# Stage 0 of an eight-stage network: softplus kept in PSUM, one scan per tile, two tiles per GpSimd product, stage 4's weights in another place, and every engine's order from a table

## The chip, the cores and the metric

The kernel runs on one core of one Trainium2 chip. The metric is the device time of one execution in microseconds. The median of three runs of the kernel before is 1385.8 us (1383.31 to 1387.94).

## The reference, cut to what matters

An activation of 8 sequences of 256 tokens with 128 features goes through four layers of two parts, so eight stages, 0 to 7, in float32. Each stage computes x = norm(x + stage(x)); the steps of that norm are "0.e", "f" and "g" below. Stage 0 is a state-space mixer and a small MLP, 1, 2, 4 and 6 are attentions of four kinds (1 with a mixture of experts behind it), 3 an MLP with binarized weights, 5 and 7 mixtures of experts. The change bears on the arithmetic of stage 0 alone:

```
u     = silu(conv(in_proj(ln(x))))            # and z, the same with other weights
delta = softplus(dt_proj(x_proj_dt(u)) + b)
B, C  = x_proj_B(u), x_proj_C(u)              # 16 states
h[t]  = exp(delta[t] * A) * h[t-1] + delta[t] * u[t] * B[t]      # 128 channels x 16 states, h = 0 before t = 0
y     = sum over states of h * C  + u * Dp
x1    = x + out_proj([y, z])
out   = x1 + (gelu(ln(x1) @ w1 + b1) @ w2 + b2)
x     = norm(x + out)
```

## The kernel before, in words

The 2048 tokens are four chunks (c = 0 to 3) of 512 tokens, two sequences of 256 each. A chunk's eight stages run one after another. Three lanes of scratch space (arena) hold the chunks in flight: chunk 0, chunk 1, and chunks 2 and 3, which share the third lane. The scratch is SBUF; the eight PSUM banks of 128 x 512 floats are given out over all stages.

Each stage is a list of steps, named like "0.st", and each step has parts, each on one engine (P is TensorE, A ScalarE, V VectorE, G GpSimd, D the DMA queue SP). `order_of_steps` runs a planner while the program is being built: with `PARTS`, an assumed duration for each part, and the tables `AHEAD`, `URGENT`, `HASTE` and `STAY` it picks one part after another, and gives each engine a fixed list and each result its bank. `OPENS` and `HELD` say from which part to which a step holds a bank. The engines then run their lists in order, and wait on semaphores for one another. What is behind a waiting instruction on an engine waits with it.

Stage 0 for one chunk: the norm (0.n), the first convolution on TensorE (0.in), B and C (0.bc, two banks evicted to SBUF by ScalarE), and softplus (0.dt, 0.ln, 0.dr, 0.du): ScalarE makes |v|, relu(v), exp(-|v|), tanh(|v|/2) and a logarithm in SBUF, VectorE corrects the rounding of 1 + exp with an add L1772 and three scalar_tensor_tensor (L1775), adds, and multiplies by u (two L1769). The product delta * u goes to DRAM (0.wr) and comes back repeated, one 128 x 512 tile for each of 16 groups of eight channels and 16 states (0.rp). For each group q GpSimd multiplies the tile by B (0.db, L2315). TensorE spreads delta over the states, four groups at a time into four banks (0.da, decays, named A to D), and ScalarE turns each into exp(delta * A) in its bank. VectorE scans (0.st): two instructions of 256 elements, one per sequence, L1946 and L1947, with the decays in PSUM and the products in SBUF. Then h is multiplied by C (0.hc), by VectorE (a L1769, h and C in SBUF) or by GpSimd (L2319) as the planner decides. TensorE sums over states (0.ac). For chunk 2 the first two groups are spread by TensorE instead of the DMA (0.rb). The end: 0.y (out projection and residual), 0.m (second norm, in place of s0(c, 2)), 0.h (w1 and gelu), 0.x on GpSimd, which adds b2 to x1 (L2336; b2 is spread over partitions by the step 0.b) and then x once more (L2340), 0.o (w2, 16 matmuls, and a VectorE add), 0.e (the norm of stage 1's input).

Line numbers that the rows show: 1064 and 1068 are TensorE's helpers for a matmul and for transposes, 1514 ScalarE's helper, 1769, 1772 and 1775 VectorE's helpers for tensor_tensor, tensor_scalar and scalar_tensor_tensor, 2328 the experts' product on GpSimd (two tiles wide in stage 5), 1010 the repeated copies, 982 the weight loads.

W[0] holds stage 0's weights from column 0, and later stage 4's: `load` of stage 4 waits in the DMA queue until the last chunk (3) has passed 0.e and until products made ahead of time for stage 4 (4.l to 4.st) are in DRAM; then it loads W[0] from column 2048 and the products into columns 0 to 2047.

Of the kernel before, what the change touches and what calls it, by code (L numbers as in the profile page):

```python
# [24 lines left out]
    [("lng", 1), ("lnb", 1), ("cxb", 1), ("czb", 1), ("dtb", 1), ("dp", 1), ("ln2g", 1), ("ln2b", 1),  # L25
     ("alog", 16), ("win", 256), ("xbc", 256), ("xdt", 128), ("dtw", 128),
# [13 lines left out]
W_AT = {3: WMAX - 1160, 2: WMAX, 4: 2048}  # L40
# [7 lines left out]
FIRST0 = 1816  # L48
# [48 lines left out]
TILED = {"0.da": "r", "0.rb": "r", "1.sc": "r", "5.bb": "r", "0.f": "r", "0.b": "r", "3.b": "r", "1.a": "r", "0.ac": "c", "1.pv": "c", "4.pv": "c",  # L97
# [36 lines left out]
HELD = {("0.ac", 0): [("Y", 0, ("0.y", 0, 0), 4, 1)], ("1.pv", 0): [("Y", 0, ("1.y", 0, 0), 8, 1)],  # L134
# [10 lines left out]
for _u in range(UNITS):  # L145
# [48 lines left out]
def stage_steps(s, c):  # L194
# [42 lines left out]
    if s == 0:  # L237
# [6 lines left out]
        add("0.du", 0, ("0.ln", 0), ("0.dr", 0))  # L244
        add("0.wr", 0, ("0.du", 0))
        add("0.in", 1, ("0.bc", 0))
        for q in range(16):
            by = "0.rb" if c == BEGIN[0] and q < BEGIN[1] else "0.rp"
            if by == "0.rb":
                if q == 0:  # L250
                    add(by, 0, ("0.du", 0))
            else:
                add(by, q, ("0.wr", 0), *([("0.ac", (q - STATES) // 4)] if q >= STATES else []))
            if q % 4:
                add("0.da", q, ("0.da", q - 1))
            else:
                add("0.da", q, ("0.du", 0), ("0.a", 0, PREP), *([("0.st", q - 3)] if q >= 4 else []))
            if by == "0.rp":
                add("0.db", q, (by, q), ("0.bc", 0))
            add("0.st", q, ("0.da", q), ("0.db", q) if by == "0.rp" else (by, 0), ("0.bc", 0), *([("0.st", q - 1)] if q else []))  # L260
            add("0.hc", q, ("0.st", q))
# [6 lines left out]
        add("0.x", 0, ("0.m", 0), ("0.b", 0, PREP))  # L268
        add("0.o", 0, ("0.x", 0), *[("0.h", j) for j in range(4)])
# [79 lines left out]
def weight_steps():  # L349

    loads = [("load", s, 0, [("f" if q else "0.e", 0, c, q) for q in OVER[s] for c in range(NC)]
# [2190 lines left out]
```

## Time and profile before

| | us |
|---|---|
| median of 3 runs | 1385.8 |
| the profiled execution | 1385.3 |
| its span, first to last instruction | 1383.5 |
| TensorE busy | 1280.2 |
| VectorE busy | 941.4 |
| ScalarE busy | 896.0 |
| GpSimd busy | 789.7 |

The mean granted TensorE clock is 0.968 of full speed. The busy times overlap: five engines work side by side, so no sum of them is the span. An instruction of an engine can seem to overlap with the next by some 80 ns; the step from start to start is then what it costs. A row "engine line waited for another" is idle time of the first ended by the second.

### The profile page before, as it was taken

What the parts mean: (1) busy time and instruction counts of PE and PEld (TensorE: products, weight loads), DVE (VectorE), ACT (ScalarE), POOL (GpSimd) and SP (SyncE); (2) the same over time, 40 slices, a digit from 0 to 9 for tenths busy, and PEclk for the clock granted to TensorE, in tenths of its full rate; (3) what the DMA queues carried; (4) which work ended last, traced back from release to release, by engine and by line L of the source; (5) the groups of instructions that cost most, each with busy time, mean ns of one, the idle gap of its engine ahead of it and who ended that gap; (6) DMA issues with size and microseconds to landing.
All of it is one profiled execution on the core that took longest, in us unless ns stands there. A gap on an engine that the chain in (4) does not pass through costs nothing.

```text
span 1383.5 us, 26286 instructions
## 1 busy us (share of the span) xinstructions
PE 1280.2 (93%) x8734; PEld 909.6 (66%) x8734; DVE 941.4 (68%) x3661; ACT 896.0 (65%) x2495; POOL 789.7 (57%) x876
## 2 busy tenths in 40 slices
PE   8577988899977889999999999999999999999997
PEld 4233655567644666677767867777777867886665
DVE  5989868677568677757563663485988659864253
ACT  6736689787474679767787676556568664775231
POOL 2998666576378556466556756355435325450534
PEclk9868899899998999999999999999999999999999
DMA  8742000101141100110010001301020030001431
GB/s 285 193 122 76 9 9 2 55 2 55 55 103 28 37 1 1 55 65 1 1 63 1 1 1 63 125 1 62 2 81 1 1 93 1 2 2 70 115 91 32
DMA packets 23109, 67.86 MB, mean 49 GB/s; under 512 B 2336, under 2 KB 9120, under 8 KB 20672
## 3 DMA queue, kind: packets, MB, share of 16 engines
q1 hardware_dynamic: 22976, 66.20, 15.2%
q8 instruction: 70, 1.15, 0.3%
q14 instruction: 63, 0.52, 0.1%
HBM read 62.85 MB, written 3.34 MB: 48 GB/s over the span
## 4 chain that ended last, share of the span: by engine, by line
PE 65%; DVE 11%; POOL 9%; ACT 8%; issue 5%; DMA 2%; SPq 0%; POOLq 0%; DVEq 0%; ACTq 0%
PE bank L1064 57%; PE bank L1068 8%; ACT arena L1514 6%; POOL arena L2315 3%; DMA arena<-cf 2%; DVE arena L1769 2%; DVE arena L2261 2%; POOL arena L2386 1%; DVE arena L2254 1%; DVE arena L2012 1%; POOL arena L2385 1%; POOL arena L2328 1%; DVE arena L1947 1%; DVE arena L2010 1%; DVE stats L1783 1%
## 5 line engine op out<-in xcount | busy, mean ns | idle before, releaser
L1514 ACT ACTIVATE arena<-arena 128x256 f32<-128x256 f32 (+4 forms) x808 | 357.9, 447 | 64.7 <-DVE arena L2012 32.5
L1514 ACT ACTIVATE arena<-bank 128x512 f32<-128x512 f32 (+3 forms) x355 | 190.7, 563 | 230.3 <-PE bank L1064 144.5
L1064 PE MATMUL bank<-XT,W 128*128 128x512 f32 (+1 forms) x752 | 290.2, 523 | 1.0 <-DVE arena L1775 0.6
L1064 PEld LDWEIGHTS bank<-W,arena 128*128 128x128 f32 x1888 | 231.5, 193 | 52.5 <-issue 39.4
L1064 PE MATMUL bank<-W,arena 128*128 128x128 f32 (+1 forms) x1888 | 243.4, 279 | 6.2 <-POOL arena L2328 3.1
L2385 POOL TENSOR_TENSOR arena<-arena 128x256 f32<-128x256 f32 x192 | 117.6, 613 | 220.8 <-DVE arena L2018 220.0
L1064 PE MATMUL bank<-arena 128*32 128x128 f32 (+8 forms) x2912 | 228.0, 336 | 16.2 <-ACT arena L1514 7.4
L2328 POOL TENSOR_TENSOR arena<-arena 128x512 f32<-128x512 f32 (+1 forms) x108 | 170.8, 1601 | 93.7 <-DVE arena L1769 39.0
L1064 PEld LDWEIGHTS bank<-arena 128*32 128x32 f32 (+4 forms) x2912 | 154.8, 153 | 81.1 <-issue 45.2
L1068 PE MATMUL bank<-CF,arena 128*128 128x128 f32 x1312 | 182.1, 279 | 23.9 <-POOL arena L2386 10.7
L2386 POOL TENSOR_TENSOR arena<-arena 128x512 f32<-128x512 f32 x192 | 199.7, 1040 | 0.0
L1068 PEld LDWEIGHTS bank<-CF,arena 128*128 128x128 f32 x1312 | 150.7, 143 | 67.1 <-issue 49.5
L1064 PE MATMUL bank<-arena,W 128*128 128x512 f32 (+3 forms) x412 | 161.1, 679 | 34.0 <-DVE arena L1947 22.0
L1064 PEld LDWEIGHTS bank<-XT,W 128*128 128x128 f32 x752 | 134.0, 190 | 83.3 <-issue 77.0
L1514 ACT ACTIVATE arena<-bank,W 128x512 f32<-128x512 f32 (+1 forms) x192 | 109.5, 616 | 67.4 <-PE bank L1064 56.0
L1514 ACT ACTIVATION_READ_ACCUMULATOR arena<-arena 128x1 f32 x768 | 145.4, 189 | 0.0
L2024 DVE COPY arena<-bank 128x512 f32<-128x512 f32 x155 | 103.2, 682 | 60.7 <-PE bank L1068 60.2
L1064 PEld LDWEIGHTS bank<-arena,W 128*128 128x128 f32 (+1 forms) x412 | 59.7, 207 | 108.4 <-issue 94.5
L1769 DVE TENSOR_TENSOR arena<-bank,arena 128x512 f32<-128x512 f32 x98 | 65.9, 686 | 84.1 <-PE bank L1064 68.8
L1514 ACT ACT_TABLE_LOAD x75 | 96.2, 1283 | 25.2 <-PE bank L1064 12.5
L2012 DVE CUSTOM_DVE_ANT_0 arena<-bank,CB 128x256 f32<-128x256 f32 x256 | 107.3, 419 | 0.0
L2010 DVE CUSTOM_DVE_ANT_0 arena<-bank,CB 128x128 f32<-128x128 f32 x256 | 73.2, 286 | 40.2 <-PE bank L1064 37.2
(138 smaller groups left out, 1700.5 us busy)
## 6 DMA issues: line engine op xcount, KB each, us to landing
arena<-rws SPq DMA_DIRECT2D x8, 2048.0 KB, 7.4
arena<-rep SPq DMA_DIRECT2D x62, 256.0 KB, 5.9
arena<-rws SPq DMA_DIRECT2D x4, 1792.0 KB, 6.6
W<-w SPq DMA_DIRECT2D x2, 2124.0 KB, 8.6
arena<-rws SPq DMA_DIRECT2D x8, 384.0 KB, 10.4
W<-w SPq DMA_DIRECT2D x1, 2692.0 KB, 9.3
XT<-wkq SPq DMA_DIRECT2D x4, 512.0 KB, 8.3
W<-w SPq DMA_DIRECT2D x1, 2005.0 KB, 15.5
```

What stands on the lines that cost most here:

```text
L1064: return e.matmul(o, lhsT, rhs, start=start, stop=stop, skip_group_check=True)
L1068: ins = e.transpose(bank[b.i][:, j * 128:j * 128 + s.shape[0]], s, cst("ident"))
L1514: return e.activation(o, a, func, **kw)
L1769: return e.tensor_tensor(o, a, b, op)
L2010: e.tensor_tensor_reduce(px[:, j * 384:j * 384 + 128], bank[b.i][:, 0:128], bias[:, 0:128], -1.0, 3.4e38, ALU.add, ALU.min, nm[:, 2 * j:2 ...
L2012: e.tensor_tensor_reduce(px[:, j * 384 + 128:(j + 1) * 384], bank[b.i][:, 128:384], bias[:, 128:384], -1.0, 3.4e38, ALU.add, ALU.min, nm[: ...
L2024: e.tensor_copy(third(s, c, n), bank[b.i][:, :]).then_inc(done[b.i], 1)
L2261: own(e.match_replace(R[:, qs], e8, src[:, qs], TAKEN))
L2315: e.tensor_tensor(h, h, s0(c, 8), ALU.mult).then_inc(has["dB"], 1)
L2328: e.tensor_tensor(h, h, w, ALU.mult).then_inc(has["gw"], 1)
L2385: e.tensor_tensor(px[:, :, 0:128], px[:, :, 0:128], rec[:, :, 0:1].to_broadcast([128, 2, 128]), ALU.mult)
L2386: e.tensor_tensor(px[:, :, 128:384], px[:, :, 128:384], rec[:, :, 1:2].to_broadcast([128, 2, 256]), ALU.mult).then_inc(has["pn"], 1)
```

## The change

What it does, part by part:

- Softplus: exp(-|v|), the three corrections and the last add are written in the PSUM bank of 0.dt, which is held until a new step 0.dc. ScalarE's 0.dc copies delta from there to SBUF, all but the first column of each sequence, where VectorE has put a zero (memset).
- One scan of 512 elements instead of two of 256: the decay at the first column of the second sequence is zero, since delta is zero there and the Exp skips these columns (`later`).
- C: evicted to SBUF as before, for GpSimd, but the bank is held until the last 0.ac, and VectorE's C product reads C from the bank.
- 0.db: one GpSimd product for two groups, 128 x 1024, B broadcast over the two. It waits for both tiles.
- 0.x and 0.b go. 0.o starts with four matmuls with a single row that put b2 in its bank, and 0.y's VectorE part has a second instruction that leaves 2x + out_proj, which is x + x1, in X, and 0.o adds that.
- Stage 4's weights lie in W[0] from column 2087 to 4519, over those of stage 0's convolution, B, C and delta; w1, w2 and others of stage 0 lie in front. The load waits for 0.in, part 1, and 0.dt of all chunks and no longer for 0.e.
- 1.km: either half may go to ScalarE or VectorE.
- The order: the planner's tables are gone. `TURNS` has 3891 turns, one for each part (negative: the second of two engines that could do it), and each engine takes its parts in the order of their turns. Banks are still given out by the same walk. `PARTS` has new numbers.

The chunks begin stage 0 in the order 2, 0, 1, 3 before and 2, 1, 0, 3 after.

```diff
-W_AT = {3: WMAX - 1160, 2: WMAX, 4: 2048}
+W_AT = {3: WMAX - 1160, 2: WMAX, 4: 4135}
-HELD = {("0.ac", 0): [("Y", 0, ("0.y", 0, 0), 4, 1)], ("1.pv", 0): [("Y", 0, ("1.y", 0, 0), 8, 1)],
+HELD = {("0.dt", 0): [("b", 0, ("0.dc", 0, 0), 1, 1)], ("0.bc", 0): [("c", 0, ("0.ac", 3, 0), 1, 1)], ("0.ac", 0): [("Y", 0, ("0.y", 0, 0), 4, 1)], ("1.pv", 0): [("Y", 0, ("1.y", 0, 0), 8, 1)],
...
-    loads = [("load", s, 0, [("f" if q else "0.e", 0, c, q) for q in OVER[s] for c in range(NC)]
+    loads = [("load", s, 0, [need for q in OVER[s] for c in range(NC) for need in ([("f", 0, c, q)] if q else [("0.in", 1, c, 0), ("0.dt", 0, c, 0)])]
...
+    turns = {g: [] for g in "PAVGD"}
+    rows = {k: iter(v) for k, v in TURNS.items()}
     for x in all_steps:
+        for p, (engines, one, other) in enumerate(x.parts):
+            turn = next(rows[x.name, x.s, x.c])
+            x.parts[p] = (engines[0], one) if turn > 0 else (engines[1], other)
+            turns[x.parts[p][0]].append((abs(turn), x, p))
+    for g in "PAVGD":
+        turns[g].sort(key=lambda y: y[0])
...
+        def later(a):
+            return a.rearrange("p (b l) -> p b l", b=2)[:, :, 1:256]
...
                 elif name in ("0.o", "3.o"):
...
+                    if s == 0:
+                        for j in range(4):
+                            mm(ps[:, j * 128:(j + 1) * 128], cst("one", 1), wt(0, "b2", 0, 1), j == 0, False)
...
-                    act(s0(c, 13), s0(c, 12), ACT.Exp, scale=-1.0).then_inc(has["sf_e"], 1)
+                    act(bank[b.i][:, :], s0(c, 12), ACT.Exp, scale=-1.0).then_inc(has["sf_e"], 1)
...
+                elif name == "0.dc":
+                    b = u("b", "0.dt", c)
+                    on.wait_ge(*after("du", "0.du", c))
+                    act(later(step0(c, 0)), later(bank[b.i][:, :]), ACT.Copy).then_inc(done[b.i], 1)
...
-                    ts(s0(c, 14), s0(c, 13), 1.0, None, ALU.add).then_inc(has["sf_f"], 1)
+                    ts(s0(c, 14), ps[:, :], 1.0, None, ALU.add).then_inc(has["sf_f"], 1)
...
-                    own(tt(step0(c, 0), s0(c, 13), s0(c, 12), ALU.add))
-                    on.wait_ge(*own.last())
-                    tt(step0(c, 1), step0(c, 0), s0(c, 6), ALU.mult).then_inc(has["du"], 1)
+                    own(e.memset(step0(c, 0).rearrange("p (b l) -> p b l", b=2)[:, :, 0:1], 0.0))
+                    own(tt(ps[:, :], ps[:, :], s0(c, 12), ALU.add))
+                    on.wait_ge(*own.last())
+                    tt(step0(c, 1), ps[:, :], s0(c, 6), ALU.mult).then_inc(has["du"], 1)
...
-                    own(e.tensor_tensor_scan(h[:, 0:256], bank[a.i][:, 0:256], h[:, 0:256], 0.0, ALU.mult, ALU.add))
-                    e.tensor_tensor_scan(h[:, 256:512], bank[a.i][:, 256:512], h[:, 256:512], 0.0, ALU.mult, ALU.add
-                                         ).then_inc(done[a.i], 1)
+                    e.tensor_tensor_scan(h, bank[a.i][:, :], h, 0.0, ALU.mult, ALU.add).then_inc(done[a.i], 1)
...
-                    tt(ring0(c, n), ring0(c, n), s0(c, 16), ALU.mult).then_inc(has["hc_v"], 1)
+                    tt(ring0(c, n), ring0(c, n), bank[cc.i][:, :], ALU.mult).then_inc(has["hc_v"], 1)
...
-                    tt(s0(c, 2), bank[b.i][:, :], rows(0, c), ALU.add).then_inc(done[b.i], 1)
+                    own(tt(s0(c, 2), bank[b.i][:, :], rows(0, c), ALU.add))
+                    stt(rows(0, c), rows(0, c), 2.0, bank[b.i][:, :], ALU.mult, ALU.add).then_inc(done[b.i], 1)
...
-                    h = ring0(c, n)
-                    on.wait_ge(*repeated(c, n))
+                    h = ar(c, 3640 + (2 * n % STATES) * 512, 1024).rearrange("p (k t) -> p k t", k=2)
+                    on.wait_ge(*repeated(c, 2 * n))
+                    on.wait_ge(*repeated(c, 2 * n + 1))
                     on.wait_ge(*emptied(u("b", "0.bc", c)))
-                    e.tensor_tensor(h, h, s0(c, 8), ALU.mult).then_inc(has["dB"], 1)
+                    e.tensor_tensor(h, h, s0(c, 8).unsqueeze(1).to_broadcast([128, 2, 512]), ALU.mult).then_inc(has["dB"], 1)
```

## Rows read from the trace of the kernel before

**Rows 1.** page: busy time per engine; tenths busy in 40 slices

```profile
PE 1280.2 (93%) x8734; PEld 909.6 (66%) x8734; DVE 941.4 (68%) x3661; ACT 896.0 (65%) x2495; POOL 789.7 (57%) x876
...
PE   8577988899977889999999999999999999999997
```

**Rows 2.** stretches: length, busy us (count) per engine, PEclk, DMA share, GB/s

```profile
20.00:150.00 130.00, 94.39 (x454) 45.27 (x453) 116.78 (x196) 80.37 (x122) 110.56 (x80) 0.83 0.48 128
150.00:200.00 50.00, 43.01 (x344) 30.55 (x347) 35.44 (x154) 39.67 (x126) 32.42 (x34) 0.86 0.03 11
200.00:385.00 185.00, 168.90 (x1376) 115.08 (x1372) 132.43 (x606) 142.13 (x446) 112.47 (x124) 0.97 0.08 32
385.00:500.00 115.00, 93.24 (x561) 63.66 (x560) 83.80 (x225) 69.47 (x136) 80.12 (x71) 0.93 0.19 51
500.00:1350.00 850.00, 837.47 (x5826) 627.33 (x5825) 552.97 (x2417) 549.49 (x1646) 434.51 (x549) 1.00 0.11 37
```

**Rows 3.** waits, 50 to 100 us: total us, times, longest

```profile
ACT bank L1514 <- PE bank L1064: 23.5, 5, 8.1
...
DVE arena L1946 <- ACT bank L1514: 4.6, 1, 4.6
```

**Rows 4.** chain of waits, in time: start us, length us, what

```profile
38.54 11.08 POOL arena L2315 x7
...
403.08 14.06 POOL arena L2315 x10
```

**Rows 5.** VectorE forms, 20 to 150 us: xcount | busy us, mean ns

```profile
L1769 DVE TENSOR_TENSOR arena<-arena 128x512 f32<-128x512 f32 x31 | 32.4, 1053 | 1.6 <-ACT arena L1514 0.7
...
L1775 DVE SCALAR_TENSOR_TENSOR arena<-arena 128x512 f32<-128x512 f32 x9 | 11.6, 1293 | 0.7
...
L1769 DVE TENSOR_TENSOR arena<-bank,arena 128x512 f32<-128x512 f32 x4 | 2.7, 674 | 4.1 <-PE bank L1064 4.1
...
L1775 DVE SCALAR_TENSOR_TENSOR arena<-arena,W,bank 128x512 f32<-128x512 f32 x2 | 1.5, 732 | 0.6 <-issue 0.6
```

**Rows 6.** timeline of VectorE: start us, length us

```profile
39.63 5.70 DVE L1769 TENSOR_TENSOR arena<-arena 128x512 f32<-128x512 f32 x4
...
58.71 0.66 DVE L1769 TENSOR_TENSOR arena<-arena 128x512 f32<-128x512 f32 x1
59.29 0.68 DVE L1946 TENSOR_TENSOR_SCAN arena<-bank,arena 128x256 f32<-128x256 f32 x1
```

**Rows 7.** GpSimd by form, 20 to 150 us

```profile
L2315 POOL TENSOR_TENSOR arena<-arena 128x512 f32<-128x512 f32 x46 | 69.3, 1535 | 0.0
L2319 POOL TENSOR_TENSOR arena<-arena 128x512 f32<-128x512 f32 x21 | 27.6, 1329 | 20.7 <-DVE arena L1947 20.7
...
L2340 POOL TENSOR_TENSOR arena<-arena,X 128x512 f32<-128x512 f32 x2 | 2.9, 1438 | 0.2
```

**Rows 8.** all forms, whole span

```profile
L2328 POOL TENSOR_TENSOR arena<-arena 128x1024 f32<-128x1024 f32 x32 | 75.1, 2365 | 10.5 <-ACT arena L1514 10.5
...
L1514 ACT ACTIVATE arena<-bank 128x512 f32<-128x512 f32 x311 | 178.4, 595 | 212.1 <-PE bank L1064 139.4 <-PE bank L1068 71.8
...
L1514 ACT ACTIVATE bank<-bank,am 128x512 f32<-128x512 f32 x64 | 44.3, 750 | 34.1 <-PE bank L1064 34.0
```

**Rows 9.** VectorE and GpSimd by form, 385 to 480 us

```profile
L1769 DVE TENSOR_TENSOR arena<-arena 128x512 f32<-128x512 f32 x12 | 12.2, 1017 | 2.0 <-ACT arena L1514 1.5
...
L2315 POOL TENSOR_TENSOR arena<-arena 128x512 f32<-128x512 f32 x16 | 22.1, 1409 | 0.4 <-DMA arena<-rep 0.4
```

**Rows 10.** timelines of the DMA queue (SPq) and TensorE

```profile
393.23 22.37 SPq L1010 DMA_DIRECT2D arena<-rep  x16
477.36 0.35 SPq L982 DMA_DIRECT2D W<-w  x1
...
49.48 2.09 PE L1064 MATMUL bank<-arena,W 32*128 32x512 f32 x8 [2.93 <-ACT arena L1514]
...
484.70 3.79 PE L1064 MATMUL bank<-bw,arena 128*128 128x128 f32 x32
```

More of the change, by code:

```diff
@@ L46 @@
 FIRST = 148
-FIRST0 = 1816
+LATE0 = 1924
 CONSTB = [("mask", 384)]
@@ L244, in stage_steps @@
         add("0.du", 0, ("0.ln", 0), ("0.dr", 0))
+        add("0.dc", 0, ("0.du", 0))
         add("0.wr", 0, ("0.du", 0))
@@ L256, in stage_steps @@
             else:
[L257 to L260, printed above, removed]
+                add("0.da", q, ("0.dc", 0), ("0.a", 0, PREP), *([("0.st", q - 3)] if q >= 4 else []))
+            if by == "0.rp" and q % 2:
+                add("0.db", q // 2, (by, q - 1), (by, q), ("0.bc", 0))
+        for q in range(16):
+            by = "0.rb" if c == BEGIN[0] and q < BEGIN[1] else "0.rp"
+            add("0.st", q, ("0.da", q), ("0.db", q // 2) if by == "0.rp" else (by, 0), ("0.bc", 0), *([("0.st", q - 1)] if q else []))
             add("0.hc", q, ("0.st", q))
@@ L267, in stage_steps @@
             add("0.h", j, ("0.m", 0))
-        add("0.x", 0, ("0.m", 0), ("0.b", 0, PREP))
-        add("0.o", 0, ("0.x", 0), *[("0.h", j) for j in range(4)])
+        add("0.o", 0, *[("0.h", j) for j in range(4)])
         add("0.e", 0, ("0.o", 0))
@@ L489, in __init__ @@
         self.parts, self.at = parts_of(name, n), 0
-        self.open, self.tail, self.since, self.behind = 0, 0.0, LANDS.get((name, c), 0.0), []
+        self.open, self.since, self.behind = 0, LANDS.get((name, c), 0.0), []
 def order_of_steps():
@@ L523, in order_of_steps @@
             x.open += 1
-    done_tails = set()
-    def tail(x):
-        stack = [x]
-        while stack:
-            y = stack[-1]
-            todo = [z for z in y.behind if z not in done_tails]
-            if todo:
-                stack += todo
-                continue
-            stack.pop()
-            y.tail = sum(p[1] + HOP[p[0][0]] for p in y.parts) + max((z.tail for z in y.behind), default=0.0)
-            done_tails.add(y)
-    for x in all_steps:
-        if x not in done_tails:
-            tail(x)
+    turns = {g: [] for g in "PAVGD"}
+    rows = {k: iter(v) for k, v in TURNS.items()}
+    for x in all_steps:
+        for p, (engines, one, other) in enumerate(x.parts):
[4 more added lines that the diff above has]
+        turns[g].sort(key=lambda y: y[0])
     order = {g: [] for g in "PAVGD"}
     free = dict.fromkeys("PAVGD", 0.0)
-    ready = {g: [] for g in "PAVGD"}
     banks = [(0.0, i) for i in range(8)]
@@ L546, in order_of_steps @@
     table, tiles = "e", "F"
-    def offer(since, x):
-        for g in x.parts[x.at][0]:
-            ready[g].append((since, x))
-    for x in all_steps:
-        if x.open == 0:
-            offer(x.since, x)
     def opened(x):
@@ L559, in opened @@
         return out + [(r, last, f, g) for r, o, last, f, g in HELD.get((x.name, x.n), ()) if o == x.at]
-    left = len(all_steps)
-    while left:
+    while any(turns.values()):
         best = None
         for g in "PAVGD":
-            for r, x in ready[g]:
-                t = max(r, free[g])
-                k = len(opened(x))
-                if k > len(banks):
-                    continue
-                if k:
-                    t = max(t, sorted(banks)[k - 1][0])
-                other = STAY["act"] if g == "A" and TABLE.get(x.name, table) != table else 0.0
-                turn = STAY["stay"] if g == "P" and tiled(x) != tiles else 0.0
-                key = (t - HASTE.get(x.name, 0.0) + other, -x.tail - AHEAD.get((x.s, x.c), 0.0)
-                       - URGENT.get(x.name, 0.0) - URGENT.get((x.name, x.c), 0.0) + turn)
-                if best is None or key < best[0]:
-                    best = key, g, t, r, x
-        key, g, t, r, x = best
-        for h in x.parts[x.at][0]:
-            ready[h].remove((r, x))
-        x.parts[x.at] = g, x.parts[x.at][1 if g == x.parts[x.at][0][0] else 2]
+            _, x, p = turns[g][0] if turns[g] else (0, None, 0)
+            if x is None or x.open or x.at != p:
+                continue
+            t, k = max(x.since, free[g]), len(opened(x))
+            if k > len(banks):
+                continue
+            if k:
+                t = max(t, sorted(banks)[k - 1][0])
+            if best is None or t < best[0]:
+                best = t, g, x
+        t, g, x = best
+        turns[g].pop(0)
         if g == "A" and x.name in TABLE:
@@ L606, in order_of_steps @@
         if x.at < len(x.parts):
-            offer(end + HOP[g], x)
+            x.since = end + HOP[g]
         else:
-            left -= 1
             for y in x.behind:
@@ L1159, in _ @@
                                  ring0(c, 4 * n + j), n == 0, n == 3)
+                        if n == 3 and j == 0:
+                            ins.then_inc(done[uses["c", "0.bc", c, 0].i], 1)
                     ins.then_inc(full[b.i], 1)
@@ L1592, in _ @@
                 elif name == "0.bc":
-                    for k, to in (("b", s0(c, 8)), ("c", s0(c, 16))):
-                        b = u(k, name, c)
-                        evict(b, to, bank[b.i][:, :])
+                    b, cc = u("b", name, c), uses["c", name, c, 0]
+                    evict(b, s0(c, 8), bank[b.i][:, :])
+                    on.wait_ge(*filled(cc))
+                    act(s0(c, 16), bank[cc.i][:, :], ACT.Copy).then_inc(has["c"], 1)
                 elif name == "0.f":
@@ L1615, in _ @@
                     on.wait_ge(*filled(a))
-                    act(bank[a.i][:, :], bank[a.i][:, :], ACT.Exp, scale=am[:, g:g + 1], bias=am[:, 16 + g:17 + g]).then_inc(has["dA"], 1)
+                    act(later(bank[a.i][:, :]), later(bank[a.i][:, :]), ACT.Exp, scale=am[:, g:g + 1], bias=am[:, 16 + g:17 + g]).then_inc(has["dA"], 1)
                 elif name == "0.h":
@@ L1642, in _ @@
                     on.wait_ge(*after("kq", "1.kq", c, 0))
-                    for i in (1, 3):
+                    for i in (n, n + 2):
                         ins = act(km1(c)[:, i * 512:(i + 1) * 512], s1(c, 3), ACT.Copy, scale=cst("hm")[:, i:i + 1])
@@ L1967, in _ @@
                     b = u("b", name, c)
-                    on.wait_ge(*after("x0", "0.x", c))
+                    on.wait_ge(*emptied(u("b", "0.y", c)))
                     on.wait_ge(*filled(b))
-                    tt(s0(c, 2), bank[b.i][:, :], s0(c, 2), ALU.add).then_inc(done[b.i], 1)
+                    tt(s0(c, 2), bank[b.i][:, :], rows(0, c), ALU.add).then_inc(done[b.i], 1)
                 elif name == "1.m" and p == 1:
@@ L1989, in _ @@
                     on.wait_ge(*after("kq", "1.kq", c, 0))
-                    for i in (0, 2):
+                    for i in (n, n + 2):
                         ins = ts(km1(c)[:, i * 512:(i + 1) * 512], s1(c, 3), cst("hm")[:, i:i + 1], None, ALU.mult)
@@ L2328, in _ @@
                     e.tensor_tensor(h, h, w, ALU.mult).then_inc(has["gw"], 1)
-                elif name in ("0.x", "3.x", "4.x", "6.x"):
-                    a = s0(c, 2) if s == 0 else rows(s, c)
-                    if s == 0:
-                        on.wait_ge(*after("z", "0.m", c))
-                    on.wait_ge(*emptied(u("b", {0: "0.b", 3: "3.b", 4: "4.b", 6: "6.b2"}[s], PREP)))
-                    if s:
-                        on.wait_ge(*xt_in(s, c))
-                    ins = e.tensor_tensor(v4(a), v4(a), bias_of(s).unsqueeze(1).to_broadcast([128, 4, 128]), ALU.add)
-                    if s == 0:
-                        own(ins)
-                        on.wait_ge(*own.last())
-                        ins = e.tensor_tensor(a, a, rows(0, c), ALU.add)
-                    ins.then_inc(has[f"x{s}"], 1)
+                elif name in ("3.x", "4.x", "6.x"):
+                    a = rows(s, c)
+                    on.wait_ge(*emptied(u("b", {3: "3.b", 4: "4.b", 6: "6.b2"}[s], PREP)))
+                    on.wait_ge(*xt_in(s, c))
+                    e.tensor_tensor(v4(a), v4(a), bias_of(s).unsqueeze(1).to_broadcast([128, 4, 128]), ALU.add).then_inc(has[f"x{s}"], 1)
                 elif name == "1.kq":
```

104 lines of the change are left out of this document (51 added, 53 removed), and 369 rows, old and new, of tables (AHEAD, EMITS, HASTE, OPENS).

## The prediction

> **What bounds the kernel now.** I read the busy shares first: TensorE works 93% of the span and stands at 9 tenths in every slice from the 16th to the last but one, while VectorE, ScalarE and GpSimd lie between 57 and 68% [rows 1]. So from about 500 us on TensorE's own work sets the end, and what is left to win lies where it idles. The view by stretches says where: it is busy 94.4 of 130 us in 20 to 150, 43.0 of 50, 168.9 of 185, 93.2 of 115, and then 837.5 of 850 [rows 2]. That is 35.6 + 7.0 + 16.1 + 21.8 + 12.5 = 93 us of idle time, 80.5 of it before 500. The two bad stretches (20 to 150, with stage 0 of chunks 2, 0 and 1, and 385 to 500, with that of chunk 3) also have a granted clock of 0.83 and 0.93, so part of TensorE's work went at the lower of its two levels there [rows 2].
>
> In 20 to 150 VectorE is busy 116.8 us and GpSimd 110.6 of 130 [rows 2]: this pair bounds stage 0. ScalarE waits 23.5 us for the decays' matmuls in 50 to 100, which in turn wait for scans to free their banks [rows 3]; the chain of waits runs through GpSimd's B products L2315, 11.1 us at 38.5 and 14.1 us at 403 [rows 4]. And the two engines slow each other down. VectorE's 512-wide product costs 1053 ns with both inputs in SBUF and 674 with one in PSUM; a softplus step costs 1293 ns, against 732 with a PSUM operand [rows 5]. It is not the SBUF read itself: in the timeline one such product takes 0.66 us at 58.71, but the four at 39.63 take 5.70, beside GpSimd's products of 11.08 / 7 = 1.6 us [rows 4, 6]. GpSimd's B product takes 1535 ns in the mean and its C product, of the same shape, 1329 [rows 7].
>
> **Stage 0 of the first three chunks, VectorE.** Of the 31 products with both inputs in SBUF [rows 5], 6 are those of softplus (two a chunk), so 25 are C products. All get a PSUM operand: 31 x (1.053 - 0.674) = 11.7 us. The nine L1775: 9 x (1.293 - 0.732) = 5.0. Sorted by turn, the new table gives VectorE 22 C products of these chunks (2, 11 and 9 of chunks 0, 1 and 2): 3 x 0.67 = 2.0. The scan: no row shows one of 512. The halves are 0.66 to 0.68 long but start about 0.6 apart, so they overlap by 0.08, as the scan at 59.29 starts before the product of 58.71 ends [rows 6]. One scan saves one such start: between nothing and 0.16 a tile, I take 0.07, for 46 tiles 3.2 us (bounds 0 and 7.4). Added: the add L1772 reads PSUM and cannot cost more than a product's 0.67; I put half of that on, 1.0 for three. The second residual of 0.y: 3 x 0.73 = 2.2. Three memsets of two columns, 0.2. Sum: 11.7 + 5.0 + 2.0 + 3.2 - 3.4 = 18.5 us off VectorE.
>
> **GpSimd.** 46 B products at 1.535 are 70.6 us [rows 7]. The two-tile ones have a row of their shape in stage 5, 2365 ns [rows 8]: 23 x 2.365 = 54.4, so 16.2 off. Bounds: 2 x 1.535 each, nothing off, if what slows them is not VectorE's second SBUF input, and 2.365 as the other end, which I take. 0.x goes: two of its three pairs lie in this stretch, four instructions of 1.44 [rows 7], 5.8 off. C products: 26 for 23, 4.0 on. Net 18.0 off.
>
> The Trainium skill, SBUF — State Buffer, section "SBUF: two separate sides", says that a VectorE instruction with two SBUF inputs and a GpSimd instruction that reads SBUF exclude each other, each for the whole of the other. The trace agrees (674 against 1053 ns). By this rule the end of 2.365 holds; if PSUM operands did not free GpSimd, the stage's gain below would be 8 us and not 16, and the sum 1366.
>
> The pair lose 18.5 + 18.0 = 36.5 us of work, 18.2 each if evenly shared, and both were nearly full. Against it: the copy of delta out of PSUM (0.dc) now stands between softplus and the decays, 0.6 us like any 512-wide eviction [rows 8], and the first tile of a chunk waits for a second copy and a product 1.0 us longer (2.365 - 1.329); for chunk 2, which starts alone, nothing hides that. I take 16 us. Since TensorE idles 35.6 us of this stretch and the work behind is TensorE's, they come off the end. Holding C and delta in PSUM costs no time by itself; its price is banks, a rival below. The Exp of the decays is as long as before (0.75 [rows 8]).
>
> **Stage 0 of chunk 3.** VectorE: twelve products at 1.017, 12 x (1.017 - 0.674) = 4.1 [rows 5, 9], three L1775 1.7, four fewer C products 2.7, scans 1.1, added 1.1: 8.5 off. GpSimd: 22.1 us of B products [rows 9] against 8 x 2.365 = 18.9, the pair of 0.x 2.9, four more C products 5.3 on: 0.8 off. Half of 9.3 is 4.6; I take 4, as TensorE has 21.8 us of idle time here and the chain ran through GpSimd.
>
> **Stage 4's weights.** The queue has issued chunk 3's copies by 415.6 (393.23 + 22.37), and the load waits until 477.4 for that chunk's last norm [rows 10]. Now it waits for the convolutions and delta only and can go right behind the copies, 60 us earlier; nothing stands behind it in the queue. Today TensorE has stage 1 of chunk 3 to do while it lands. In the new table stage 4 of chunks 0 and 1 opens right behind chunk 3's 0.o, which the old gate would have stalled. Alone the move is worth 0 to 6 us (a quarter of the 21.8 idle): I take 3.
>
> **TensorE's own additions.** Sixteen matmuls of 128 columns for b2. An output of 16 matmuls (32 records) takes 3.79 us [rows 10], 0.237 each: 3.8 on, 0.3 off for 0.b, all on the path: +3.5.
>
> **The order.** Chunk 1 now comes before chunk 0 in stage 0, and evictions are shared anew (59 of stage 1's 96 probability evictions on VectorE, 34 of stage 6's). The third chunk leaves stage 0 at TensorE's 92nd turn, before at the 95th, so the same work fills that stretch. A better order can reach the idle time not yet counted, 16.1 + 21.8 + 12.5 - 7 = 43 us. From 500 on TensorE already runs at 98.5% and in 200 to 500 at 87% [rows 2]. Bounds: 28 gained (two thirds of it) and 20 lost (2.4% of the 837 us given back). I take 8 gained, a fifth of the idle time of 200 to 500 and nearer to no effect than to either end, as no row shows the new order.
>
> **Sum.** The profiled execution took 1385.3 us (span 1383.5); the median of the runs is 1385.8. -16 - 4 - 3 + 3.5 - 8 = -27.5, so 1385.3 - 27.5 = 1357.8, say 1358.
>
> **Rivals.**
> 1. The order is worth more and fills two thirds of the idle time, 28 instead of 8: 1338. For it: 80 us of idle lie before 500, and the gate of stage 4 falls. Against: at the start there is no other work to fill with.
> 2. The pair's gain is absorbed and the order does nothing: TensorE waits for ScalarE instead, whose Exps stay as they are. A gain of 4 to 8, less 3.5: about 1382, hardly to be told from no change.
> 3. Slower: banks. C holds one bank per chunk through the whole scan, three with three chunks in flight; delta holds one until 0.dc, Y one. That leaves three or four of eight, so the four decay tiles of a group cannot be made while the last four are scanned. Each group then exposes its matmuls (2.09) and an Exp (0.75) [rows 8, 10], 2.9 us. The profile shows such a hand-over once, VectorE idle for 4.6 us behind ScalarE [rows 3]. Twelve groups in three chunks: 35 us over the forecast, 1393. It decides from ten groups on (27.5 / 2.9). Against it: another chunk's scans can stand in between.
> 4. The two-tile product is no cheaper: 1366, within the forecast's own range.
>
> **Chances.** Forecast with 4, a gain of 13 to 40 us: 0.58 (its own range 1345 to 1372). Rival 1: 0.16. Rival 2: 0.13, half of it within 0.3%. Rival 3: 0.13, a little of it within 0.3%. 0.3% or 4.2 us is about what a measurement of this kernel can tell. Faster 0.58 + 0.16 + 0.06 = 0.80, same 0.08, slower 0.12. The range runs from 1330 (20 off in the first stretch, 6, 5, 28 for the order, 3.5 on) to 1386, which leaves out most of rival 3.
>
> **What would show it.** No 128x512 product with both inputs in SBUF should be left on VectorE in stage 0, and the C product should cost 0.67 us; the two-tile product 2.4; the single scan 1.1 to 1.3. GpSimd should leave most of the chain before 100 us. TensorE's idle time in 20 to 150 should fall from 35.6 to about 20 us, and stage 4's load should be issued right behind chunk 3's copies. The forecast is wrong if TensorE waits for a bank in every group, if the two-tile product takes 3 us, or if the idle time from 200 on grows.

## The result, and the profile after

The changed kernel takes 1342.9 us (median of 4 runs, 1341.0 to 1346.8), the kernel before 1386.5 on the same chip: ratio 0.969, 95% interval 0.966 to 0.972, some 43 us less. The forecast was 1358 (1330 to 1386), with 0.80 on faster: the direction and the stated range held. The gain came out 16 us larger than summed, and the time lies below the 1345 to 1372 that the forecast's own mechanism was given, 5 us from rival 1's 1338; what that means for rival 1 is said at the end. The profiled execution has a span of 1340.4 us and a mean granted clock of 0.977; before it was 1383.5 and 0.968.

The page after: busy time by engine, TensorE's tenths in 40 slices, and the chain that ended last.

```profile
PE 1270.5 (95%) x8764; PEld 902.9 (67%) x8764; DVE 912.6 (68%) x3585; ACT 905.4 (68%) x2518; POOL 768.3 (57%) x844
...
PE   8779988999997989999999999999999999999997
...
PE 76%; DVE 10%; ACT 5%; issue 3%; DMA 3%; POOL 2%; SPq 0%; POOLq 0%; DVEq 0%; ACTq 0%
```

The same by stretches (length, busy us and count of PE, PEld, DVE, ACT, POOL, then the granted clock):

```profile
20.00:150.00 130.00, 108.01 (x546) 54.46 (x545) 104.26 (x183) 92.67 (x150) 97.11 (x61) 0.83 0.47 130
150.00:200.00 50.00, 44.37 (x404) 31.01 (x406) 44.15 (x207) 47.25 (x168) 35.46 (x40) 0.93 0.02 7
200.00:385.00 185.00, 173.97 (x1401) 121.45 (x1400) 138.71 (x572) 136.78 (x399) 121.42 (x129) 1.00 0.08 31
385.00:500.00 115.00, 99.15 (x649) 65.98 (x648) 86.75 (x270) 73.32 (x171) 73.51 (x70) 0.97 0.20 51
500.00:1340.00 840.00, 827.54 (x5723) 619.63 (x5721) 528.84 (x2315) 546.14 (x1622) 437.29 (x540) 1.00 0.12 38
```

TensorE's idle time is the length less its busy time. Against [rows 2] it fell from 35.6 to 22.0 in 20 to 150, from 7.0 to 5.6, 16.1 to 11.0 and 21.8 to 15.9; over the whole span from 103.3 (1383.5 - 1280.2) to 69.9. That is 33.4 of the 43.1 us. The other 9.7 are TensorE's busy time, which fell although b2's matmuls came on; the mean granted clock rose from 0.968 to 0.977, which goes with less of its work at the lower level, but no run separates the two. GpSimd's share of the chain fell from 9% to 2%.

VectorE and GpSimd in 20 to 150 (count, busy us and mean ns of one, idle time before it and what ended that), which answer [rows 5] and [rows 7]:

```profile
L2089 DVE TENSOR_TENSOR_SCAN arena<-bank,arena 128x512 f32<-128x512 f32 x48 | 56.2, 1208 | 11.0 <-ACT bank L1649 10.7 <-POOL arena L2459 0.3
L1910 DVE TENSOR_TENSOR arena<-arena,bank 128x512 f32<-128x512 f32 x22 | 14.3, 673 | 0.1
L1916 DVE SCALAR_TENSOR_TENSOR bank<-arena,bank 128x512 f32<-128x512 f32 x6 | 4.2, 696 | 0.4
```

```profile
L2459 POOL TENSOR_TENSOR arena<-arena 128x1024 f32<-128x1024 f32 x23 | 53.6, 2348 | 2.9 <-DMA arena<-rep 2.9
L2463 POOL TENSOR_TENSOR arena<-arena 128x512 f32<-128x512 f32 x26 | 32.6, 1266 | 26.4 <-DVE arena L2089 26.4
```

The C product costs 0.67 us, the two-tile product 2.35, the single scan 1.21, a softplus step 0.70: each at its forecast or within 5% of it. GpSimd's C product, an instruction that the change left alone, fell from 1329 ns to 1266.

The DMA queue after, against [rows 10]: stage 4's weights go right behind chunk 3's copies, at 418.9 and not 477.4.

```profile
396.80 21.86 SPq L1137 DMA_DIRECT2D arena<-rep  x16
418.90 0.39 SPq L1105 DMA_DIRECT2D W<-w  x1
419.39 0.38 SPq L1179 DMA_DIRECT2D W<-gs  x1
```

### The profile page after: what moved, and what is told of

Its sections match the earlier page's. It is cut to its first block, busy times and chain, and to the rows that moved or that the text cites. A ratio compares the mean times of both kernels' runs of the same rounds, so it can differ in the third digit from the quotient of the medians.

```text
span 1340.4 us, 26157 instructions
## 1 busy us (share of the span) xinstructions
PE 1270.5 (95%) x8764; PEld 902.9 (67%) x8764; DVE 912.6 (68%) x3585; ACT 905.4 (68%) x2518; POOL 768.3 (57%) x844
## 4 chain that ended last, share of the span: by engine, by line
PE 76%; DVE 10%; ACT 5%; issue 3%; DMA 3%; POOL 2%; SPq 0%; POOLq 0%; DVEq 0%; ACTq 0%
PE bank L1191 66%; PE bank L1195 10%; ACT arena L1649 5%; DVE arena L1910 2%; DVE arena L2089 2%; DMA arena<-cf 2%; DVE arena L2155 1%; DVE stats L1924 1%; DVE arena L2153 1%; DVE stats L1913 1%; ACT L1649 0%; DVE arena L1913 0%; ACT bank L1649 0%; DVE stats L1927 0%; DVE bank L1916 0%
## 5 line engine op out<-in xcount | busy, mean ns | idle before, releaser
L1649 ACT ACTIVATE arena<-arena 128x256 f32<-128x256 f32 (+2 forms) x804 | 355.8, 448 | 44.5 <-DVE arena L2155 24.5
L1649 ACT ACTIVATE arena<-bank 128x512 f32<-128x512 f32 (+2 forms) x376 | 199.1, 564 | 205.6 <-PE bank L1191 131.6
L1191 PE MATMUL bank<-XT,W 128*128 128x512 f32 (+1 forms) x752 | 294.4, 524 | 0.4 <-DVE arena L2155 0.4
L1191 PEld LDWEIGHTS bank<-W,arena 128*128 128x128 f32 (+1 forms) x1888 | 227.3, 192 | 35.7 <-issue 27.8
L1191 PE MATMUL bank<-W,arena 128*128 128x128 f32 (+2 forms) x1888 | 237.9, 276 | 3.6 <-POOL arena L2472 2.7
L1191 PE MATMUL bank<-arena 128*32 128x128 f32 (+8 forms) x2912 | 225.3, 336 | 10.9 <-DVE arena L2155 2.9
L1195 PE MATMUL bank<-CF,arena 128*128 128x128 f32 x1312 | 184.5, 279 | 13.6 <-ACT arena L1649 5.5
L1191 PE MATMUL bank<-arena,W 128*128 128x512 f32 (+3 forms) x412 | 156.6, 651 | 25.2 <-DVE arena L2089 14.7
L2167 DVE COPY arena<-bank 128x512 f32<-128x512 f32 x140 | 93.5, 682 | 50.2 <-PE bank L1195 49.5
```

What stands on the lines that cost most here:

```text
L1191: return e.matmul(o, lhsT, rhs, start=start, stop=stop, skip_group_check=True)
L1195: ins = e.transpose(bank[b.i][:, j * 128:j * 128 + s.shape[0]], s, cst("ident"))
L1649: return e.activation(o, a, func, **kw)
L2167: e.tensor_copy(third(s, c, n), bank[b.i][:, :]).then_inc(done[b.i], 1)
```

## The experiments

Two theories were put to the test. T1: the instruction forms relieve VectorE and GpSimd in stage 0, and most of the 43 us is that. T2: the table of turns fills TensorE's idle time, and most of it is that. All are edits of the changed kernel; medians of 4 to 6 runs, each beside runs of the kernel before (medians 1385.4 to 1386.4). The changed kernel itself was not run again beside them; its four runs spread from 1341.0 to 1346.8, with a ratio of 0.966 to 0.972. So a run whose interval overlaps that one (e4, e6, e8, e11) is not told apart from the changed kernel, whatever its median says.

| | us | against changed (1342.9) | ratio to before, 95% |
|---|---|---|---|
| e1 old instruction forms | 1364.5 | +21.7 | 0.983 to 0.988 |
| e2 the planner's order | 1453.5 | +110.6 | 1.047 to 1.052 |
| e3 C product from SBUF | 1361.4 | +18.6 | 0.981 to 0.985 |
| e4 two products of 512 | 1343.9 | +1.0 | 0.969 to 0.973 |
| e5 e3 with e4 | 1355.1 | +12.2 | 0.975 to 0.980 |
| e6 two scans | 1345.4 | +2.5 | 0.968 to 0.973 |
| e7 later load of stage 4 | 1352.9 | +10.0 | 0.974 to 0.979 |
| e8 without b2 | 1344.6 | +1.7 | 0.966 to 0.973 |
| e9 e1 with e7 | 1373.4 | +30.5 | 0.989 to 0.992 |
| e10 softplus in SBUF | 1359.2 | +16.3 | 0.979 to 0.982 |
| e11 four C products moved | 1345.7 | +2.8 | 0.968 to 0.973 |

**e1, the old forms in the new order** (the edits of e3, e4, e6 and e10 together). It does not bring back 0.x and 0.b: b2 stays with TensorE's matmuls, and C and delta hold their banks as in the changed kernel.

> The changed kernel's order, banks and stage 4 load, with the instructions of stage 0 as they were: softplus in SBUF, VectorE's C product with both inputs in SBUF, two scans of 256, two products of 512 by B (issued in one turn), the Exp of the decays over the whole width. Two theories. T1, the instruction forms: VectorE and GpSimd got shorter work in stage 0, and that is most of the 43 us. Then the time goes back by 18 to 28 us, to 1361 to 1371, TensorE idles 33 us or more of 20 to 150 us (22 now), and the stretches from 385 us on keep their gain except for chunk 3's 4 us. T2, the order: the table fills TensorE's idle time, and the forms only relieve two engines that were not the limit. Then the time stays at 1343 to 1353 and TensorE's idle time in 20 to 150 rises by less than 6 us. In both the C product of VectorE goes back to 1.0 us and GpSimd's product to 1.5.

It lost 21.7 us, half of the gain: T1 for this half. Where it was lost:

```profile
20.00:150.00 130.00, 93.71 (x429) 45.92 (x428) 108.66 (x173) 79.27 (x121) 99.24 (x72) 0.80 0.48 128
...
385.00:500.00 115.00, 99.86 (x599) 66.86 (x598) 88.93 (x235) 68.52 (x126) 80.28 (x72) 0.99 0.18 51
```

TensorE idles 36.3 us of 20 to 150, as before the change (35.6): with the old forms this table of turns fills nothing there, and putting them back costs all 14 us of idle time that the change took out of this stretch. It does not follow that the forms do this alone; e2 has a number for that. In 385 to 500 it keeps its gain (15.1).

**e2, the changed instructions under the planner of before.**

```
-    rows = {k: iter(v) for k, v in TURNS.items()}      # and the sort by turn
+    # order_of_steps, AHEAD, URGENT, HASTE, STAY of the kernel before
```

> The changed kernel's instructions, with each engine's order computed by the planner of the kernel before from its costs, instead of read from the table of turns. T1, the forms: TensorE's idle time in 20 to 150 us stays near 22 to 26, the time is 1350 to 1360. T2, the order: 1368 to 1380, and the idle time of 385 to 500 us is back at 20 and that of 500 to the end above 18. My forecast's own terms (forms and load 19.5 net, order 8) say 1366 for this run if they are all of the effect, 16 less in all than was measured; if e1 and this run together lose more than 43 us against the changed kernel, forms and order need each other.

Neither theory said this: 68 us slower than before. It is not the order of before with new instructions, since the planner chose anew, with tables set for other steps and banks. In 20 to 150 TensorE idles 33.1 us and waits 23.4 of them for scans (19.2 before the change, 12.2 in the changed kernel). From 500 on it idles 62 us, where before it idled 20 (12.5 up to 1350 [rows 2] and 7.6 behind it). The wait (us in total, times, longest), then the two stretches:

```profile
PE bank L1074 <- DVE arena L1972: 23.4, 8, 7.4
```

```profile
20.00:150.00 130.00, 96.93 (x473) 51.55 (x472) 88.81 (x137) 83.92 (x125) 87.53 (x52) 0.83 0.50 132
...
500.00:1448.00 948.00, 885.79 (x5990) 654.90 (x5988) 565.38 (x2476) 575.15 (x1699) 456.94 (x569) 0.97 0.10 34
```

By the expectation's own test (e1 and e2 together lose 132 us, and not 43) forms and order need each other: in 20 to 150 TensorE idles 36.3 us with the new table alone, 33.1 with the new forms under this planner, 22.0 with both. The run does not say how much an order is worth, and which wait makes the 111 us is not shown. The old order itself was not run with the new forms. By my count along its turns it could not be: C of three chunks, one delta and one Y hold five banks at the first decays of chunk 0, which open four. That would be rival 3 of the prediction, but it is a count that no run shows.

**e3, VectorE's C product reads C from SBUF.**

```
-    tt(ring0(c, n), ring0(c, n), bank[cc.i][:, :], ALU.mult)
+    tt(ring0(c, n), ring0(c, n), s0(c, 16), ALU.mult)
```

> The changed kernel with one operand changed: VectorE's C products of stage 0 read C from SBUF instead of the PSUM bank; order, banks and everything else stay. T1 (the two engines shut each other out of SBUF): VectorE's C product costs 1.05 us or more instead of 0.67, GpSimd's two-tile product rises above 2.35 us, and the time rises by 4 to 10 us (28 products, 0.38 us each, 10.6 us of VectorE, a third to all of it on the path). T2 (VectorE has slack): less than 3 us. If the C product stays under 0.75 us, the SBUF read is not what made it long before.

More than either bound: 18.6 us for one operand. The 22 C products of 20 to 150 are 754 ns longer each (1427 against 673), and chunk 3's six 430 (1101 against 671): 19.2 us of VectorE, so nearly all of it lies on the path, where the expectation had half the price and a third to all of it. **e4** splits the two-tile product, and **e5** does both:

```
-    e.tensor_tensor(h, h, s0(c, 8).unsqueeze(1).to_broadcast([128, 2, 512]), ALU.mult)
+    e.tensor_tensor(h[:, 0, :], h[:, 0, :], s0(c, 8), ALU.mult)
+    e.tensor_tensor(h[:, 1, :], h[:, 1, :], s0(c, 8), ALU.mult)
```

> The changed kernel with GpSimd's product of two tiles by B split into two products of 512, one behind the other in the same turn. By the trace of before 1.535 us each, 3.07 for 2.35, 0.7 us in each of 23 steps of the first three chunks and 8 of chunk 3: 22 us of GpSimd in all. T1: with VectorE's operands in PSUM a product of 512 costs about 1.25 us, as GpSimd's C product does now (1266 ns), so the pair costs 2.5, and the time rises by 1 to 4 us. If instead the form itself was the gain: 3.0 a pair and 8 to 12 us. T2: no change, under 2 us.

> The changed kernel with both edits of e3 and e4: VectorE's C product reads C from SBUF, and GpSimd's two-tile product is two of 512. With C in PSUM the split cost 1.0 us (e4). Theory L, the two engines shut each other out of SBUF for the whole of an instruction: VectorE's C product, 1427 ns beside a product of 2551 ns in e3, waits only for a shorter one and comes to about 1060 ns as in the kernel with all old forms, so that the split now gains: 22 products x 0.37 us = 8 us of VectorE in the first 160 us, and 3 to 8 us of the time, 1353 to 1358. Rival S, the SBUF read is slow by a fixed amount: the C product stays at 1.4 us and the time at 1361 to 1363.

VectorE's C product and GpSimd's B product in 20 to 150, of e3, then of e5:

```profile
L1910 DVE TENSOR_TENSOR arena<-arena 128x512 f32<-128x512 f32 x22 | 30.9, 1427 | 0.1
L2458 POOL TENSOR_TENSOR arena<-arena 128x1024 f32<-128x1024 f32 x23 | 58.2, 2551 | 1.4 <-DMA arena<-rep 1.4
```

```profile
L1910 DVE TENSOR_TENSOR arena<-arena 128x512 f32<-128x512 f32 x22 | 24.3, 1125 | 0.1
L2459 POOL TENSOR_TENSOR arena<-arena 128x512 f32<-128x512 f32 x23 | 31.8, 1384 | 0.0
```

The excess over 673 ns is 754 ns beside products of two tiles and 452 beside those of one: it goes with the length of the other engine's instruction (theory L, whose range of 1353 to 1358 held), and a fixed cost of the SBUF read is out. With C in SBUF the split gains 6.4 us; with C in PSUM its 1.0 us is not told from nothing, but it is well short of the 8 to 12 us of "the form itself was the gain". The two halves cost 2 x 1271 ns in e4 against 2348: the wide form by itself saves 0.2 us a pair. The rest of the 0.7 us that the prediction gave it went with VectorE's second SBUF operands: with them back, the halves cost 1366 and 1384 ns in e5 and 1419 and 1559 in e1.

**e6, two scans of 256.**

```
+    own(e.tensor_tensor_scan(h[:, 0:256], bank[a.i][:, 0:256], h[:, 0:256], 0.0, ALU.mult, ALU.add))
```

> The changed kernel with two scans of 256 instead of one of 512. By the traces 672 + 661 ns less an overlap of 0.08 against 1208: 0.05 to 0.12 us a tile, 64 tiles, 3 to 8 us of VectorE, of which 46 tiles lie in the first 150 us. T1, VectorE bounds stage 0: the time rises by 1 to 5 us. T2: less than 1 us.

+2.5 us lies in T1's range, but it is not told apart from nothing by these runs; the halves take 673 and 661 ns against 1208 for the whole.

**e7, the load of stage 4 gated by 0.y.**

```
-    on.wait_ge(*emptied(u("b", "0.in", c, 1)))
-    on.wait_ge(*filled(u("b", "0.dt", c)))
+    on.wait_ge(*emptied(u("b", "0.y", c)))
```

> The changed kernel with stage 4's load waiting for the first step of every chunk's 0.y (Y's bank emptied) instead of for the convolutions and delta: about 20 to 25 us later. My forecast gave the earlier load 3 us (bounds 0 and 6). Theory O (the new order makes use of it, as stage 4 of chunks 0 and 1 opens right behind chunk 3's stage 0): the load lands 20 us later, TensorE idles longer in 430 to 480 us, the time rises by 3 to 10 us. Rival: the products that need these weights have slack, and the time stays within 1 us.

10.0 us, the upper end of theory O (five runs, 1349.6 to 1356.7). The load goes 27 us later (446.07), and TensorE waits for it; the timeline around it, of e7 and then the same matmuls in the changed kernel:

```profile
442.66 2.02 PE L1190 MATMUL bank<-W,arena 128*128 128x128 f32 x16
451.31 0.79 PE L1190 MATMUL bank<-W 128*128 128x128 f32 x2 [6.63 <-DMA W<-gs]
452.03 0.79 PE L1190 MATMUL bank<-W,CF 1*128 1x128 f32 x2
452.75 3.78 PE L1190 MATMUL bank<-XT,bw 128*128 128x512 f32 x4
...
461.75 3.70 PE L1190 MATMUL bank<-arena,W 128*128 128x512 f32 x8 [0.87 <-ACT arena L1648]
```

```profile
441.46 2.02 PE L1191 MATMUL bank<-W,arena 128*128 128x128 f32 x16
443.32 0.39 PE L1191 MATMUL bank<-W 128*128 128x128 f32 x2
443.63 0.48 PE L1191 MATMUL bank<-W,CF 1*128 1x128 f32 x2
444.05 1.98 PE L1191 MATMUL bank<-XT,bw 128*128 128x512 f32 x4
...
451.17 3.70 PE L1191 MATMUL bank<-arena,W 128*128 128x512 f32 x8 [0.87 <-ACT arena L1649]
```

The wait is 6.6 us, and the work behind it runs at half speed (3.78 against 1.98): the granted clock fell to its lower level after the idle time, 0.64 in 450 to 460 and 1.00 in the changed kernel. Followed along the two timelines, e7 is 1.2 us behind the changed kernel ahead of the wait (442.66 against 441.46), 8.0 behind it (451.31 against 443.32) and 10.6 once the slow work is done (461.75 against 451.17), which is also the difference of the spans. So the load is worth 9.4 us in these traces, 6.8 by the wait and 2.6 by the clock; the first 1.2 arise before the load is due, behind a clock of 0.52 in 410 to 420 (1.00 in the changed kernel).

**e8, without the sixteen matmuls of b2** (the result then lacks b2).

```
-    mm(ps[:, j * 128:(j + 1) * 128], cst("one", 1), wt(0, "b2", 0, 1), j == 0, False)
```

> The changed kernel without the sixteen matmuls that add b2 to stage 0's outputs; the output lacks that bias. My forecast put them at 3.8 us (16 x 0.237), all on the path. The trace of the changed kernel has four of them in 1.15 us, 4.6 in all. If they are all on the path, the time falls by 3.5 to 4.6 us; if those of the first three chunks lie in TensorE's idle time, by 1 to 2 us.

No gain in the median. But its six runs lie in two groups by granted clock: 1337.2 and 1337.8 at 0.979 and 0.978, 1348.0 to 1349.6 at 0.973 to 0.970, one between. The fastest is 3.8 us below the changed kernel's fastest (1341.0 at 0.978), what the forecast gave these matmuls, but that compares one run with one run. The profiled run is of the longer group, with half the clock for all of 410 to 420; below it the changed kernel there, and then e4:

```profile
410.00:420.00 10.00, 10.00 (x49) 9.02 (x48) 6.35 (x17) 0.00 (x0) 9.51 (x6) 0.50 0.22 50
```

```profile
410.00:420.00 10.00, 7.86 (x64) 5.19 (x64) 9.67 (x20) 5.17 (x9) 10.00 (x6) 1.00 0.33 85
```

```profile
410.00:420.00 10.00, 10.00 (x47) 8.46 (x46) 6.53 (x17) 0.00 (x0) 9.27 (x8) 0.50 0.06 17
```

The drop does not come from leaving b2 out: the profiled runs of e4, e6 and e7, which keep its matmuls, also have a clock of 0.50 to 0.52 in 410 to 420, those of the changed kernel and e11 have 1.00. So medians of four to six runs also count how often it fell, which is one reason why e4, e6, e8 and e11 are not told apart. Whether b2's matmuls make it rarer stays open.

**e9, old forms and late load** (the edits of e1 and e7 together).

> All old instructions of stage 0 (as e1) and stage 4's load waiting for 0.y (as e7): what is left of the change is the order of the turns, the banks and b2's matmuls. Singly the forms gave back 21.7 us (e1) and the load 10.0 (e7). If the parts add up, this is 1364.5 + 10.0 = 1374.5 us, and the order with b2 is worth 12 us against 1386. If the load only mattered because the shorter forms bring chunk 3's stage 0 forward, this stays at 1364 to 1368 and the order is worth some 20. If it goes to 1380 or above, order and load need each other.

1373.4: the parts add up within 1.2 us. What is left of the change here is worth 1386.4 - 1373.4 = 13.0 us. That is the order with its banks, but also b2's matmuls with the absence of 0.x, the freer choice in 1.km, and what the load still gains on its old place, as e7's gate gives back 27 of its 58 us. No run separates these.

**e10, softplus in SBUF.**

```
-    own(stt(ps[:, :], s0(c, 14), 1.0, ps[:, :], ALU.subtract, ALU.subtract))     # and the other steps; 0.dc copies one column
+    own(stt(s0(c, 15), s0(c, 14), 1.0, s0(c, 13), ALU.subtract, ALU.subtract))
```

> The changed kernel with the steps of softplus on SBUF operands as before and the Exp of the decays over the whole width; the copy after softplus is of one column only; C product, scan and two-tile product as changed. By the trace of the kernel with all old forms three of these steps a chunk cost 1.31 instead of 0.70 us and the add of one 1.14 instead of 0.68: 2.9 us of VectorE a chunk, less the copy's 0.6 on ScalarE. My forecast priced them at 5.0 + part of the rest for three chunks. Theory: they stand in a serial chain ahead of each chunk's first decays, so nearly all of it shows for chunk 2 and chunk 3: +1 to +4 us. Rival: under 1 us, since VectorE's other chunks' work fills in.

Expected +1 to +4, measured +16.3: both theories missed. The timelines of VectorE and GpSimd in e10, then VectorE in the changed kernel:

```profile
32.77 8.21 DVE L1916 SCALAR_TENSOR_TENSOR arena<-arena 128x512 f32<-128x512 f32 x3
32.40 8.03 POOL L2456 TENSOR_TENSOR arena<-arena 128x1024 f32<-128x1024 f32 x3
```

```profile
32.79 1.50 DVE L1916 SCALAR_TENSOR_TENSOR bank<-arena,bank 128x512 f32<-128x512 f32 x2
34.32 0.70 DVE L1916 SCALAR_TENSOR_TENSOR bank<-bank,arena 128x512 f32<-128x512 f32 x1
```

Three steps in 8.21 us beside three products in 8.03: one of each by turns, 2.7 us a round, where the same steps take 2.2 us in all in the changed kernel. My expectation had taken 1.31 us a step from e1, where GpSimd's products are half as long. These 6 us stand in front of everything that chunk 2 still has to scan: in 35 to 50 TensorE is busy 4.6 us of 15, against 10.0. So e3 and e10 each lose nearly as much as e1, which undoes both. One reason is that e1 also splits the product that makes them dear: e5 shows it for the C product (18.6 us to 12.2), and the nine steps of softplus cost 1788 ns in the mean here and 1309 in e1. Softplus in SBUF with the product split was not run, so how much of this is the split, and how much that the two losses overlap, stays open.

**e11, four C products of chunk 2 on VectorE.**

```
-    ("0.hc", 0, 2): (48, -49, 69, 71, -118, -85, 92, -115, 106, -130, ...
+    ("0.hc", 0, 2): (48, -49, 69, 71, 118, 85, 92, 115, 106, 130, ...
```

> The changed kernel with four C products of chunk 2 moved from GpSimd to VectorE in their turns (0.67 us each instead of 1.27). In the trace GpSimd is busy 43 of the 45 us from 50 to 95 us, VectorE 36. If GpSimd bounds that stretch, 5.1 us come off it and 2.7 go on VectorE: 1 to 3 us faster than the changed kernel, 1340 to 1342. If the chain is VectorE's scans, 1 to 3 us slower. If the split is balanced, within 1 us.

1342.3 to 1348.8 against 1341.0 to 1346.8: not told apart. The 1 to 3 us faster or slower of the expectation are less than these runs can show, so that the split is near balance is likely and not shown. By its median no version beats the changed kernel.

## Why the prediction was right, and where its sizes were off

- **What bounds the kernel** held: TensorE from 500 us on, VectorE with GpSimd in stage 0. Neither theory alone was right: undoing the forms gives back 21.7 us of 43.6, and by e2 forms and order need each other. So the sizes below are what undoing each in the changed kernel costs, and not what each would gain by itself.
- **Stage 0, VectorE and GpSimd (-16, and -4 for chunk 3)**: 20 against 21.7 by e1 and 20.5 by e9 with e7 (1373.4 - 1352.9). The 20 also held the removal of 0.x and the new split of C products, which e1 leaves as they are; for the first three chunks what e1 undoes is 18.7 of VectorE and 16.2 of GpSimd by the forecast's own prices, 34.9 of its 36.5, so the comparison is fair. The idle time of TensorE in 20 to 150 fell by 13.6 us. The 4 us of chunk 3 are not seen by themselves: TensorE idles 15.1 us of 385 to 500 in e1 and 15.9 in the changed kernel. The price of 2.365 for the two-tile product was right (2.348). Of the 16.2 us that it takes off GpSimd, the form itself gives 0.19 a pair, 4.5; the rest comes from VectorE's PSUM operands, as the forecast's own sentence on the end of 2.365 had it. The rule of the Trainium skill, page SBUF — State Buffer, section "SBUF: two separate sides", that such instructions hold each other up for a whole instruction, agrees with e3, e5 and e10: 1427, 1125 and 2737 ns for one instruction of VectorE. It shows most plainly in e10, where steps and products take turns; the other two are means over instructions that met a product and some that met none. What I did not draw from it is that the two-tile product makes every VectorE instruction with two SBUF inputs that is left dearer: its excess was 754 ns instead of 452.
- **Rival 1** (the order fills 28 us instead of 8: 1338) is nearest to the measured time, but not by its mechanism: e9 leaves 13.0 us for the order with all that e9 cannot part from it, half of the rival's 28. The time came there because the load and the order were both under-priced. That it still lay in the stated range is owed to the wide bound of the order term, which was set at 28 by choice and not by a row.
- **Rival 4** (two-tile product no cheaper) fell by its row, 2348 ns.
- **Stage 4's weights (-3, bounds 0 and 6)**: mis-sized. e7, which takes back only 27 of the 58 us, costs 10.0, and 8.8 with old forms (e9 less e1). The bound of 6 was "a quarter of the 21.8 idle"; the wait alone is 6.6, and the slower clock behind it was not in the sum.
- **b2's matmuls (+3.5)**: the fastest runs differ by that much (3.8), the medians do not (e8's is 1.7 higher); open. What the absence of 0.x gave in return was not run.
- **The order (-8)**: mis-sized. With b2 it was forecast at -4.5 and e9 shows -13.0, so 13 to 17 for the order and the banks, if b2's matmuls cost 0 to 4 and the rest that e9 leaves in is small. Compared with [rows 2], e1 idles 6.7 us less in 385 to 500, with the early load, and 6.7 less in 500 to 1310 (5.8 against 12.5), and nothing less in 20 to 150. That "at the start there is no other work to fill with" agrees with e1 for this table; later the idle time was easier to fill than the fifth that I took.
- **Rivals 2 and 3** did not come. TensorE's wait for the scan's banks in 20 to 150 is 12.2 us (19.2 before), and VectorE's wait for ScalarE 10.7: 5.0 before: of the hand-over of banks that rival 3 priced at 35 us, about 6 came on. In e2 TensorE's wait for the scan's banks is 23.4 us.

The terms by the runs: forms 21, load 9 to 10, order with banks, b2 and what else e9 leaves in 13, together 43 to 44. The last is what remains by subtraction and was not run by itself. The forecast had 20, 3 and 4.5.

## What to carry to other kernels

Where GpSimd and VectorE share a stage, look first for VectorE instructions with two SBUF inputs, and price each at its own time plus part of the GpSimd instruction beside it: a PSUM operand is worth more the longer that instruction is, so the two edits belong together (e3, e5, e10). An early load is worth not its own wait alone but also the slower clock behind that wait (e7). An order made for one set of instructions and banks is not an order for another (e2): measure forms and order by undoing each in the changed kernel, and do not expect the pieces to add up (e3 and e10 against e1).

## What the runs showed of the hardware that was not expected

- A scalar_tensor_tensor of 128 x 512 on VectorE with both inputs in SBUF took 2.74 us in the mean of three beside GpSimd products of 128 x 1024, 0.70 with a PSUM operand, and 1.31 in the mean beside products of 128 x 512 (e1).
- GpSimd's product of 128 x 1024 took 2348 ns with no such neighbour, and 2551 with it (e3); two of 128 x 512 took 2 x 1271 (e4).
- A scan over 512 columns took 1208 ns, its two halves 673 and 661.
- After TensorE's wait of 6.6 us, four matmuls of 512 columns took 3.78 us and not 1.98 (e7). The same code ran at 1337.2 and at 1349.6 us, with mean granted clocks of 0.979 and 0.970 (e8). In 410 to 420 the profiled runs of e4, e6, e7 and e8 had a clock of 0.50 to 0.52, those of the changed kernel and e11 1.00.
